# An early-fusion transformer block over eight images: per-image stages replaced by one list-scheduled order over all images

## The reference, cut to what matters

```python
# 8 images of 518x518x3; 32x32 patches of 16x16, 128 features; 77 text rows: 1101 rows of 128 each
h = L0_tok(x)                 # shifted patches, conv 16x16 -> 128, layernorm, dense
h = concatenate([h, txt], axis=1)
h = h + attn(layernorm(h))    # 8 heads of 64, causal mask, softmax over 1101 keys
h = h + ffn(layernorm(h))     # "sparse" attention, 8 heads of 16:
#   x += depthwise conv of 3 along the rows; q,k,v = x @ qkv_w.T + qkv_b
#   idx = top_k(q k^T, 16); softmax over those 16 keys; weighted sum of v; @ wo_w.T + wo_b
```

## Time and profile before

| | |
|---|---|
| median of 3 runs | 5569.98 us (5568.24 to 5572.65) |
| profiled execution | 5581.88 us, of which span 5580.1 us |
| mean granted TensorE clock | 0.84 of full speed |
| PE / PEld busy | 3848.1 us (69%) / 2582.3 us (46%) |
| DVE busy | 3808.6 us (68%) |
| ACT / POOL busy | 2759.8 us (49%) / 2839.3 us (51%) |

### The profile page before, as it was taken

How to read it: one execution, slowest core, us unless ns; L and a number is a source line. 1 busy time by engine, 2 the same in 40 slices (tenths; PEclk the granted TensorE clock), 3 DMA queues, 4 the chain that set the end, 5 groups by cost and what they waited for, 6 DMA issues and landing times.

```text
span 5580.1 us, 86720 instructions
## 1 busy us (share of the span) xinstructions
PE 3848.1 (69%) x32347; PEld 2582.3 (46%) x32632; DVE 3808.6 (68%) x5374; ACT 2759.8 (49%) x6137; POOL 2839.3 (51%) x3474
## 2 busy tenths in 40 slices
PE   4675777667777577757777577766777757773666
PEld 3444444444445344454444444444444534442444
DVE  1224887657874778738787488755788467873997
ACT  1442565435653456525565266543566346651444
POOL 2221666426663466616666166642666246661665
PEclk8877998878988789878998789887898878986676
DMA  3023001030201202030020300103020110003000
GB/s 52 3 30 50 3 9 24 5 51 2 31 1 27 28 3 31 1 53 2 3 31 1 54 3 11 21 5 50 2 31 1 33 22 2 3 1 51 1 1 5
DMA packets 221488, 103.25 MB, mean 19 GB/s; under 512 B 183616, under 2 KB 198544, under 8 KB 221072
## 3 DMA queue, kind: packets, MB, share of 16 engines
q1 hardware_dynamic: 221072, 97.68, 11.8%
HBM read 78.98 MB, written 18.67 MB: 17 GB/s over the span
## 4 chain that ended last, share of the span: by engine, by line
DVE 37%; PE 34%; ACT 13%; issue 7%; DMA 6%; POOL 2%; SPq 2%; DVEq 0%; ACTq 0%; POOLq 0%
PE causal_ps L716 10%; DVE A L1136 9%; DVE top L1131 9%; DVE top L1141 7%; PE out_ps L807 6%; ACT PB L998 6%; PE causal_ps L784 4%; DVE negmax L1153 4%; DMA H<-in_txt 4%; DVE A L1145 4%; PE logit_ps L742 3%; PE out_ps L835 2%; PE causal_ps L752 2%; ACT E L987 2%; ACT PT L932 2%
## 5 line engine op out<-in xcount | busy, mean ns | idle before, releaser
L601 POOL TENSOR_TENSOR A<-A,E 128x1101 f32<-128x1101 f32 x576 | 1378.9, 2394 | 0.8 <-issue 0.7
L1131 DVE MAX8 top<-logit_ps 128x8 f32<-128x1101 f32 x576 | 752.8, 1307 | 703.6 <-PE logit_ps L742 703.3
L932 ACT ACTIVATE PT<-causal_ps 128x512 f32<-128x512 f32 (+1 forms) x1728 | 820.7, 486 | 811.7 <-PE causal_ps L716 810.6
L716 PE MATMUL causal_ps<-ident,A 128*128 128x128 f32 (+1 forms) x5184 | 1031.6, 322 | 256.9 <-ACT PT L932 132.3
L590 POOL TENSOR_SCALAR A<-A 128x1101 f32<-128x1101 f32 x576 | 645.0, 1120 | 694.1 <-DVE A L1145 682.6
L716 PEld LDWEIGHTS causal_ps<-ident,A 128*128 128x128 f32 (+1 forms) x5184 | 681.0, 162 | 638.9 <-ACT PT L932 298.4
L987 ACT ACTIVATE E<-logit_ps,negtop 128x1101 f32<-128x1101 f32 x576 | 680.3, 1181 | 550.9 <-DVE A L1136 548.0
L595 POOL TENSOR_SCALAR negtop<-top 128x1 f32<-128x1 f32 x576 | 110.7, 192 | 1495.4 <-DVE top L1131 1469.6
L1141 DVE MAX8 top<-A 128x8 f32<-128x1101 f32 x576 | 753.2, 1308 | 11.3
L1136 DVE MATCH_REPLACE8 A<-top,logit_ps 128x1101 f32<-128x1101 f32 x576 | 746.0, 1295 | 0.9 <-issue 0.9
L1145 DVE MATCH_REPLACE8 A<-top,A 128x1101 f32<-128x1101 f32 x576 | 743.1, 1290 | 0.0
(11 more groups left out here) (140 smaller groups left out, 4127.9 us busy)
## 6 DMA issues: line engine op xcount, KB each, us to landing
stack<-qk_parts SPq DMA_DIRECT2D x128, 288.0 KB, 19.8
X<-in_x SPq DMA_DIRECT2D x248, 121.5 KB, 4.4
qk_parts<-OT SPq DMA_DIRECT2D x16, 864.0 KB, 5.2
Wp<-in_L_attn_W_in SPq DMA_DIRECT2D x96, 64.0 KB, 2.1
out<-H SPq DMA_DIRECT2D x8, 512.0 KB
stack<-in_L_tok_conv_w SPq DMA_DIRECT2D x30, 64.0 KB, 2.4
X<-in_x SPq DMA_DIRECT2D x8, 108.0 KB
H<-in_txt SPq DMA_DIRECT2D x8, 38.5 KB
```

Source lines behind the costliest of these rows:

```text
L601: nc.gpsimd.tensor_tensor(A[:, t % 3, :], A[:, t % 3, :], E1[:, t % 2, 0:L], ALU.add).then_inc(chosen, 1)
L716: last = nc.tensor.transpose(bank[0:w, 128 * j:128 * j + 128], src, ident[:, :])
L932: nc.scalar.activation(PT[0:rows, t % SLOTS, 512 * j:512 * j + 128 * len(tiles)], bank[0:rows, 0:128 * len(tiles)], ACT.Relu).then_inc(tur ...
L1131: nc.vector.max(top[:, t % 3, 0:8], logit_ps[:, 0:L]).then_inc(top8, 1)
```

## The change

The cycles, the hand-made rounds and `drained` go. A planner (`Plan`, `make_plan`) lists every piece of work of all eight images as an event with an engine, a planned duration, a due time and the events that it must follow; `arrange` plays these forward and, whenever an engine is free in that play, gives it the ready event that is due first. The five resulting lists are the five instruction streams. Waits are on semaphores as before, so planned durations and due times only set the order on each engine.

Due times are counted in `STEP = 6.3` us for a tile, so `IMAGE = 72 * 6.3 = 453.6`. Tokens of an image are due 30 steps before its causal part starts; causal work of image c+1 and sparse work of image c are due side by side; projections, splits and stacking follow the causal part.

To make this free of overwrites, buffers are parted:

- PSUM: `logit_ps` (3 banks) for logits only, `score_ps` (2) for scores only, and 3 single banks `bank_ps` which the planner hands out to everything else, also to the sums. Projections, copies and residual work go by groups of at most 4 blocks.
- SBUF: `X1`, `x2T`, `xpT`, `XT`, `PTc`, `PT`, `E1` and `Os` each have a place of their own; `H1` and `Wp` have two buffers; `X` has 3 slots in place of 8; `stack` holds three quarters of an image (2 heads each), loaded in four parts for an image; the scratch in memory has two halves.

Work that changes its engine, all off DVE: the normalisation (L1101) becomes a tensor_scalar with two factors on POOL, with one more small DVE instruction (`shift`) for each layernorm; the conv bias (L1108) becomes one more row of the weights; the dense bias, both residual adds and the wo bias (L1113, L1120, L1122, L1198), the division (L1179) and the splits (L1212, L1215, L1217) go to POOL; the first part of the depthwise conv (L1201) goes to ACT. POOL's clearing of halos (L573) goes, since images are loaded without the halo: 8 DMAs for a block of patches in place of 4.

The 72 matmuls of a batch's sums are one event on PE, with no other work between them.

```diff
-def round_events(sparse, causal):
...
+STEP = 6.3
+IMAGE = TILES * STEP
...
+class Plan:
...
+    def add(self, engine, us, due, event, *behind, opens=None, closes=None, lag=0.12, long=False):
...
+def make_plan():
...
+        for t in range(TILES):
...
+            due = s0 + t * STEP
+            first = due - 2 * STEP
+            add("PE", 0.5, first, ("logits", c, t), ("stack", c, t // QUARTER),
+                *([("exp_all", *tile(1))] if n else []))
+            add("DVE", 1.31, first, ("first", c, t), ("logits", c, t))
+            add("DVE", 1.38, first, ("strike", c, t), ("first", c, t),
+                *([("turn_sparse", *tile(3), 2)] if n >= 3 else []))
...
+            if t % BATCH == BATCH - 1:
+                b = t // BATCH
+                add("PE", 2.8, due + 3, ("sum_sparse", c, b, 2),
+                    *[("copy_sparse", c, t - g, j) for g in range(BATCH) for j in range(3)],
...
+                    opens=("sums_s", c, b), closes=True, long=True)
...
+PLAN = make_plan()
+ORDER = PLAN.arrange()
...
-                        for k in range(3 * third, 3 * third + 3):
+                    for k in range(NT):
                             rows = LAST if k == NT - 1 else 128
                             for g in range(BATCH):
...
-            def drained(c):
-
-                pe.wait_ge(turn_free, TURNS[c, "end"])
...
-            for c in range(B + 1):
-                if c < B:
-                    tokens(c)
-                begin(c)
-                rounds(c)
-                drained(c)
-                if c > 0:
-                    output(c)
-                if c < B:
-                    projections(c, c == 0)
+            for e in ORDER["PE"]:
+                event, c, *of = e
+                if event == "turn_x":
...
```

More of the change, by code:

```diff
@@ L38, with __init__, push, pop @@
 K_PARTS = [0, 1, 0, 1, 2, 0, 2, 1]
[L41 to L58, removed]
+class Heap:
+    def __init__(self, items=()):
+        self.items = sorted(items)
+    def push(self, item):
+        a, lo, hi = self.items, 0, len(self.items)
+        while lo < hi:
+            mid = (lo + hi) // 2
+            if a[mid] < item:
+                lo = mid + 1
+            else:
+                hi = mid
+        a.insert(lo, item)
+    def pop(self):
+        return self.items.pop(0)
+    def __bool__(self):
+        return bool(self.items)
+    def first(self):
+        return self.items[0]
 HALF = 512
@@ L65 @@
 BATCH = 4
+BATCHES = TILES // BATCH
 SLOTS = BATCH + 1
-PAIR_STEPS = TILES // NP
+X_SLOTS = 2
+STACKS = 3
+QUARTER = TILES // 4
 PB_SLOTS = 4
 PT_SLOTS = 4
[L70 to L77, removed]
+BANKS = 3
+WG = [list(range(g, min(g + 4, NT))) for g in range(0, NT, 4)]
 def pieces(i):
@@ L88, in groups @@
     return [[(k, hh) for k in range(i + 1)[2 * g:2 * g + 2] for hh in range(2)] for g in range((i + 2) // 2)]
-def round_events(sparse, causal):
[L94 to L150, removed]
-            else:
[L152 to L214, removed]
@@ L217 @@
[L217 to L226, removed]
-    for c in range(B + 1):
[L228 to L254, removed]
+def last_turn(i, j):
+    return min(2 * j + 1, len(groups(i)) - 1)
@@ L477, in patches @@
                 start = x_flat[b].offset + (row * IMG * CH + j0 * P * CH - CH + e0)
-                return bass.AP(x.tensor, start, [[P * CH, G - j0], [IMG * CH, rows], [1, e1 - e0]])
-            def load_images(c, first=False):
-                for i in range(NPT):
-                    if not first:
-                        buf, n = fill(("XT", i), c - 1)
-                        sp.wait_ge(ring_done[buf], n + 1)
+                return bass.AP(x.tensor, start, [[P * CH, j1 - j0], [IMG * CH, rows], [1, UV - e0]])
@@ L634, in _ @@
-            for c in range(B + 1):
-                if c < B:
-                    halos(c)
-                rounds(c)
-        def fill_wait(pe, name, c):
-            buf, n = fill(name, c)
-            pe.wait_ge(ring_free[buf], n + 1)
-            return ring[buf], ring_done[buf]
-        def chunks(start, width):
-            cuts = [start] + [x for x in range(HALF, 3 * HALF, HALF) if start < x < start + width] + [start + width]
-            return list(zip(cuts, cuts[1:]))
+                pool.wait_ge(total_g, small[0])
@@ L651, in _, with chunks, turn @@
         @block.tensor
         def _(pe):
-            def transposes(dst, src_of, n, rows=128):
-                for t in range(n):
-                    last = nc.tensor.transpose(dst[0:rows, 128 * t:128 * t + 128], src_of(t), ident[:, :])
+            def chunks(start, width):
+                cuts = [start] + [x for x in range(HALF, 3 * HALF, HALF) if start < x < start + width] + [start + width]
+                return list(zip(cuts, cuts[1:]))
+            def turn(where, srcs):
+                for j, src in enumerate(srcs):
+                    w = src.shape[-1]
+                    last = nc.tensor.transpose(where[0:w, 128 * j:128 * j + 128], src, ident[:, :])
@@ L1220, in _, with settle @@
-            for c in range(B + 1):
-                if c < B:
-                    tokens(c)
-                rounds(c)
-                if c > 0:
-                    output(c)
-                if c < B:
-                    projections(c)
+            nc.vector.tensor_tensor(woB[:, :], bank_ps[0][:, 0:D], woB[:, :], ALU.add).then_inc(setup_done, 1)
+            small = {"ln": 0, "max": 0}
+            def settle(ins):
+                ins.then_inc(ln_v, 1)
+                small["ln"] += 1
+                dve.wait_ge(ln_v, small["ln"])
```

1666 lines of the change are left out of this document (1029 added, 637 removed).

## The result

The kernel after took **5135.4 us** (median of 4 runs, 5127.3 to 5142.2), the kernel before 5569.1 beside it: a ratio of 0.922 [0.921, 0.924]. That is faster, as forecast, but by 434 us where 1150 were forecast, and far above the range. The profiled execution took 5133.5 us with a span of 5131.7.

The account below looks back on a forecast made before the run. DVE was taken to bound each middle image: 486 us plus 22 of waits, 508. Start 448 + 7 x 508 + last image 427 = 4431 us of span, 10 less for the median: 4420 us, range 4250 to 4720.

Parts of the forecast that it names:

- The start: Time until the first sparse logits: 115 + 263 + 10 + 45 + 8 + 7 = 448 us.
- tokens of image 0 need 115 us: First step of the start: 100 us now, plus some for three X slots, smaller groups and normalisation on POOL.
- the sum: Whole kernel: start 448, seven images of 508 each, last image 427, together 4431 us of span.
- P = 508: Time of each of the seven middle images: 486 us of DVE work plus 22 us of waits.
- 22 us for all waits: DVE's remaining waits in a middle image, mainly for logits, taken between 8 and 90 us; unbroken sums included.
- the 89% of 508 named as a sign: Sign in the middle of the kernel: DVE should be busy near 89% of each 508 us image.
- The last image: Sparse work alone and the tail, taken as unchanged: 411 + 16 = 427 us.
- Rival 2: Some 41 two-input DVE instructions an image wait for POOL passes: 28 us an image, P = 536, total 4627; chance 0.17.
- The unbroken sums: 72 matmuls of a batch without break on PE: between 7 us gained and 47 us lost, for 18 batches.
- Rival 1: Middle images: list order hides all waits and DVE is full, P = 486 to 490, total 4284; chance 0.2.
- Rival 3: Middle images: only the 107 us without rounds go, P stays 554 to 560, total 4795; chance 0.1.
- Rivals 4 and 5: Whole kernel: 4, single buffers keep stages serial, 5570, chance 0.01; 5, PE held at low clock, 5992, chance 0.02.

Follow-up runs that it names:

- n32: Kernel after with each image row loaded by one 32-partition DMA, left halo column not cleared: 4463.5 us, ratio 0.800.
- n32_neg: n32 with one more planner edge, placing POOL's long add of a tile behind the next tile's negation: 4355.7 us, ratio 0.780.
- experiment 4: Timed row-maxima combinings beside POOL in the kernel after, then took the 192 combinings out of n32: 4343.8 us, ratio 0.778.
- best: Kernel after with 32-partition image DMAs, halo clearing, sums in three pieces, no combining of row maxima, negation before the add: 4243.5 us, ratio 0.760.

## Why the prediction failed, by its own steps

**The start, 453 of the 701 us.** The step that failed is "tokens of image 0 need 115 us (100 now, plus some for three slots of `X`, smaller groups and normalisation on POOL)". It took the loads as they are now, and the diff changed them: eight transfers for a block of patches in place of four, the large ones over 31 partitions. In the kernel after the first causal scores stand at 375.1 us, 260 late. From there to the first load of the stack (L757, 889.9 us) it took 515 us where the sum had 326, another 189 (the last 4 come behind it): the tokens of image 1 lie in PE's list between the pieces of causal work, and 160 us of PE's wait for `X` fall in this stretch. The sum took the causal part as undisturbed by them. It counts the DMAs of the stack and not those of `X`. `n32`, which brings the shape back, starts at 425 us, 23 under the forecast: its first causal scores stand at 105.4 us (115 forecast), its first load of the stack at 412.4 (115 + 263 + 10 + 45 + 8 = 441), and the first maximum comes 12.6 us behind it (7).

**The seven images, 200 us.** P = 508 measured 536.6 in the kernel after and 509 in `n32`. So the difference was again the loads. The wait for logits was 90 us, I had 22 us for all waits, and the stage of `n32` from 2460 to 2975 shows 14.4:

```profile
DVE top L1424 <- PE logit_ps L1088: 14.4, 16, 2.5
```

But the agreement of 508 with 509 is in part luck, for it hides errors that cancel. Without gaps and waits the forecast has DVE busy 380.6 + 54 + 18 = 453 us of an image, the 89% of 508 named as a sign; `n32` has 472.8 on average over the seven (93%). Of the 20 more, the combining's stretch is 24 x (0.715 - 0.16) = 13. Against that, gaps and waits took 36 us an image where the sum had 55. In the mixed stages of the kernel after and of `n32`, the last of each left out, PE was busy 410 to 431 us at 0.91 to 0.98, where I had 445 at 0.9 and 418 at full clock; POOL 380 to 387 against 385, ACT 340 to 350 against 360.

**The last image, 47 us.** "The last image is as now: 411 + 16" was wrong: the work is as before (DVE 380.5 us busy, before 380.6) but its order isn't. I took over the time of a stage whose instructions are the same, and didn't ask in what order the planner would list them. With the one edge of `n32_neg` the last image took 4350.7 - 3920.3 = 430 us, against the 427 forecast.

**Rival 2, right in kind.** I gave it 0.17 and left it out of the sum, since the trace of before never shows the pair side by side. The pair does exclude: 0.16 us became 0.71 on average, 1.00 beside a POOL instruction and 0.16 where none ran. I had 28 us for an image, 196 in the seven, for all 41 instructions; the 192 combinings, 24 an image, are worth 120 us with the instructions themselves. The rule of the Trainium skill, page "SBUF — State Buffer", section "Who interferes with whom", agrees with this trace, and with its 67 and 125 combinings of experiment 4. A chance of 0.17 was low for a mechanism with a stated rule and no row against it. That this rival's P of 536 is the measured 536.6 is chance: the loads make up 28 us of it, and without them an image takes 509.

**The unbroken sums.** Bounds were a gain of 7 and a loss of 47 us an image. Measured: 17 us over the whole run for the piece itself, 2 us an image; DVE's cover hides nearly all, as I said. The 0.2 us for each break, on which the gain of 7 rests, stand in no row, and no run measured them. That the altered plan would be worth more than the piece (39 us from 2.8 to 2.6) I had not thought of.

**The other rivals.** Rival 1 (DVE full, 4284) is not what the change gave, though `best` passes it. Rival 3 (P of 554 to 560) is near the 536.6 by number, but not by cause: the wait for logits was 117.7 us in the first mixed stage of the kernel after, while loads were late, and 14.4 in the one of `n32` shown. Rivals 4 and 5 fell: the stages overlap, and the mean clock rose from 0.84 to 0.88.

**What I could have read beforehand.** The rule on this shape stands in the Trainium skill, page "DMA: Bandwidth & Descriptors", section "Why a DMA increments its semaphore by 16 and not by 1": a transfer is spread over the largest number of DMA engines, 16 at most, that divides the slowest dimension on both sides. 32 partitions give 16 engines by it and 31 give one. The measurements agree: 7.3 us for a pair at 31 and a DMA share of 0.08, half a microsecond of issue at 32 and a share of 0.65. No view here lists the engines of a single transfer.

## What to carry to other kernels

When a change touches how a load is cut, price every new transfer's partition count before anything else; 31 and 1 in place of 32 cost 672 us here, more than the 434 that the change gained with it, and a long issue in the profile points at the transfer ahead of it. In a list made by a planner, read the order on each engine for short instructions that another engine waits for, standing behind long ones; one edge took the last image from 475 to 430 us. Before a change of under 1% in such a list is called good or bad, move a planned duration a little: 2.6 for 2.8 us alone gave 0.9% here, so the piece itself must be tested with the list held fixed.

## What the runs showed that I had not expected

- A transfer of 117.7 KB over 31 partitions holds its queue for about 7.2 us; the same rows over 32 partitions are issued in 0.50 us. The waiting is booked on the next issue of the queue, even one of 3.6 KB.
- A DVE instruction on 128x2 elements stretches from 0.16 to 2.33 us beside a POOL add. Single-input DVE `TENSOR_SCALAR` of nine columns (L1366) is stretched as well, from 172 ns before to 731 after, which I had not counted among those at risk. The timeline shows the same pattern: the 13 that start while POOL runs nothing took 0.17 us each, the 11 beside a POOL instruction 1.39 on average, and 9 of these end with it. No run takes them out.
- PE's granted clock in the start rose from 0.65-0.78 to 0.93-0.97 when its inputs came in time, so late loads cost clock as well as waiting.
